# One fused VectorE instruction per score row, joint GpSimd additions and a VectorE minimum in place of TensorE mask products, in a causal attention layer

## What is computed

```python
q = (x @ Wq + bq).reshape(Bv, Tv, N_HEAD, HEAD_DIM)      # HEAD_DIM 8
k = (x @ Wk + bk).reshape(Bv, Tv, N_HEAD, LATENT)        # LATENT 64
v = (x @ Wv + bv).reshape(Bv, Tv, N_HEAD, LATENT)
qc = jnp.einsum('bthd,dl->bthl', q, Wc)
att = jnp.einsum('bthl,bshl->bhts', qc, k) * SCALE
causal = jnp.tril(jnp.ones((Tv, Tv), dtype=bool))
att = jnp.where(causal[None, None], att, -jnp.inf)
att = jax.nn.softmax(att, axis=-1)
y = jnp.einsum('bhts,bshl->bthl', att, v).reshape(Bv, Tv, N_HEAD * LATENT)
return y @ Wo + bo
```

## Time and profile before

| What | us |
|---|---|
| median of 3 runs | 3065.84 (3062.51 to 3071.13) |
| span of the profiled execution, first to last instruction | 3008.7 |
| busy in the span: PE / DVE / ACT / POOL | 2506.9 / 2417.9 / 1891.9 / 1257.2 |
| causal pairs, first to last GpSimd addition | 1344.5 to 1959.4 |
| in it, GpSimd additions (L1526) | 572.3 |
| in it, VectorE mask additions and maxima (L1775, L1777) | 150.8 and 388.0 |

### The profile page before, as it was taken

One profiled execution on the slowest core, in us unless ns is written; L12 is line 12 of the kernel. 1 busy time (PEld: TensorE's weight loads), 2 busy tenths in 40 slices (PEclk: granted clock), 3 DMA queues, 4 the chain that ended last, 5 costly groups with the idle time before them and its releaser, 6 DMA issues. The chain is left out here.

```text
span 3008.7 us, 44190 instructions
## 1 busy us (share of the span) xinstructions
PE 2506.9 (83%) x13254; PEld 1086.0 (36%) x13254; DVE 2417.9 (80%) x4200; ACT 1891.9 (63%) x3760; POOL 1257.2 (42%) x1704
## 2 busy tenths in 40 slices
PE   6897799999999899969999999996846566666666
PEld 4544122222222354424444444375821111111366
DVE  7777888888888467878888888776459999999963
ACT  2213688888888521226666666604649999999864
POOL 2015433433334101529999999911732121200036
PEclk9999899999999899979999999996979999999879
DMA  4002322222233200642222222254221111111123
GB/s 101 1 1 88 93 75 74 74 74 74 75 106 108 58 1 1 209 158 81 82 87 87 88 89 89 81 210 137 78 80 42 44 41 43 42 43 32 36 73 90
DMA packets 193930, 229.15 MB, mean 76 GB/s; under 512 B 55824, under 2 KB 122128, under 8 KB 193248
## 3 DMA queue, kind: packets, MB, share of 16 engines
q1 hardware_dynamic: 158960, 193.15, 20.0%
q0 software_dynamic: 31360, 30.05, 3.9%
q10 hardware_dynamic: 3376, 3.15, 0.4%
HBM read 139.72 MB, written 87.95 MB: 76 GB/s over the span
## 5 line engine op out<-in xcount | busy, mean ns | idle before, releaser
L1349 DVE TENSOR_REDUCE neg_max<-ps 128x1 f32<-128x1024 f32 x512 | 602.0, 1219 | 98.7 <-PE ps L1242 90.4
L1322 ACT ACTIVATE prob<-ps 128x512 f32<-128x512 f32 x1024 | 556.3, 601 | 94.3 <-PE ps L1256 85.6
L2650 DVE TENSOR_REDUCE neg_max<-ps 128x1 f32<-128x1024 f32 x512 | 581.0, 1211 | 13.8 <-PE ps L2444 13.7
L1526 POOL TENSOR_TENSOR acc<-acc,prob 128x384 f32<-128x384 f32 (+1 forms) x630 | 572.3, 952 | 34.3 <-PE ps L1620 33.2
L2520 ACT ACTIVATE ps<-ps,neg_max 128x1024 f32<-128x1024 f32 x512 | 557.4, 1091 | 23.9 <-DVE neg_max L2650 23.0
L2444 PE MATMUL ps<-k_stack,q_stack 128*128 128x512 bf16 x1024 | 332.9, 413 | 236.7 <-ACT ps L2520 216.0
L1734 ACT ACTIVATE prob<-ps 128x512 f32<-128x512 f32 (+3 forms) x640 | 270.6, 474 | 216.0 <-PE ps L1608 159.1
L1777 DVE TENSOR_REDUCE neg_max<-ps 128x1 f32<-128x512 f32 (+7 forms) x512 | 388.0, 758 | 17.5
L1256 PE MATMUL ps<-q_stack,k_stack 128*128 128x512 bf16 x1024 | 312.2, 386 | 7.1 <-DMA k_low<-k_parts 4.9
L1266 PE MATMUL ps<-prob,v 128*32 128x512 f32 x2048 | 281.3, 621 | 0.9 <-ACT prob L1322 0.7
L2444 PEld LDWEIGHTS ps<-k_stack,q_stack 128*128 128x128 bf16 x1024 | 62.6, 99 | 501.8 <-ACT ps L2520 423.2
(11 more groups left out here) (365 smaller groups left out, 3932.7 us busy)
## 6 DMA issues: line engine op xcount, KB each, us to landing
q_stack<-q_parts SPq DMA_DIRECT2D x576, 48.0 KB
k_stack<-k_parts SPq DMA_DIRECT2D x576, 48.0 KB
o_quads<-o_out SPq DMA_DIRECT2D x64, 256.0 KB
v<-v_wide SPq DMA_DIRECT2D x32, 512.0 KB
o_pairs<-o_out SPq DMA_DIRECT2D x64, 256.0 KB
num<-o_pairs SPq DMA_DIRECT2D x8, 2048.0 KB, 8.5
q_parts<-parts SPq DMA_DIRECT2D x24, 384.0 KB, 2.5
k_parts<-parts SPq DMA_DIRECT2D x24, 384.0 KB, 2.7
```

Source lines behind the costliest of these rows:

```text
L1322: nc.scalar.activation(prob[:, m % RING, :], ps[:, bank(m), :], ACT.Exp).then_inc(exped.sem, 1)
L1349: nc.vector.tensor_reduce(neg_max[:, i.slot(2), m:m + 1], ps[:, first:first + 2, :].rearrange("p b n -> p (b n)"), AX.X, ALU.max, negate=T ...
L1526: op_of.tensor_tensor(sums, sums, weights(j, u, h), ALU.add).then_inc(added_for(j, h).sem, 1)
L2650: nc.vector.tensor_reduce(neg_max[:, n % 2, qt:qt + 1], ps[:, first:first + 2, :], AX.XY, ALU.max, negate=True).then_inc(maxed.sem, 1)
```

## The change

First, a row's mask and maximum become one VectorE instruction, `tensor_tensor_reduce`: it adds a strip (`mask_strip`, 1024 columns: zeros, and the triangle in the last 128) over the row's whole width, writes the row back and puts the negated maximum out through the accumulator. Second, GpSimd adds both heads of a unit in one instruction, so 10 additions of twice the size stand where 20 stood. Third, the products with `mask_kq` are gone. The exponential of a triangle is therefore taken unmasked, and VectorE afterwards takes the minimum of it and `cap_kq` (`cap`: 0 where the key is later than the query, a huge number elsewhere), both heads at once, eight per pair. The products with the values and the additions of such a unit wait for the cap (`capped`) instead of for the exponential. For room in SBUF, `xn` of the projection now shares memory with `o_out`.

```diff
-    for m, sign in ((S.mask_qk, -1), (S.mask_kq, 1)):
-        c.run(nc.gpsimd.memset(m[:], 0.0))
-        c.run(nc.gpsimd.affine_select(out=m[:], in_=m[:], compare_op=ALU.is_ge, fill=MASKED, base=0,
+    c.run(nc.gpsimd.memset(S.mask_strip[:], 0.0))
+    c.run(nc.gpsimd.memset(S.cap_kq[:], -MASKED))
+    for m, sign, fill in ((S.mask_strip[:, SEQ - P:SEQ], -1, MASKED), (S.cap_kq[:], 1, 0.0)):
+        c.run(nc.gpsimd.affine_select(out=m, in_=m, compare_op=ALU.is_ge, fill=fill, base=0,
...
-    xn = sb("xn", [P, 2, GROUP])
+    xn = sb("xn", [P, 2, GROUP]) if xn_room is None else xn_room
...
+    BOTH = slice(0, 2)
+    diagonals = [u for u, (kt, c) in enumerate(units) if kt * P >= c * GROUP]
+    CAPS = len(diagonals)
+    caps_after = {1: (0,), 4: (2,), 6: (4,), 9: (6,), 12: (8, 9), 15: (10,)}
+    adds_after = {6: (2, 4), 9: (4, 6), 12: (6, 8), 15: (8, 10)}
+
+    def wait_for_weights(eng, j, u, h):
+
+        if u in diagonals:
+            capped.wait(eng, j.times(CAPS, diagonals.index(u)))
+        else:
+            exped.wait(eng, j.times(2 * NU, 2 * u + h))
...
-    def add(eng, op_of, j, u, h):
+    def add(eng, op_of, j, u, heads):
         kt, c = units[u]
-        exped.wait(eng, j.times(2 * NU, 2 * u + h))
+        last = 1 if heads == BOTH else heads
+        wait_for_weights(eng, j, u, last)
...
-                op = nc.tensor.matmul(ps[:, bank(t, j.c), o:GROUP], ks[j.slot(4)][:, h, kt * P:(kt + 1) * P],
-                                      qs[j.slot(4)][:, h, c * GROUP + o:(c + 1) * GROUP], start=True,
-                                      stop=not diagonal)
-                if diagonal:
-                    op = nc.tensor.matmul(ps[:, bank(t, j.c), o:o + P], S.ident_b[:], S.mask_kq[:],
-                                          start=False, stop=True)
-                op.then_inc(s2_mm.sem, 1)
+                nc.tensor.matmul(ps[:, bank(t, j.c), o:GROUP], ks[j.slot(4)][:, h, kt * P:(kt + 1) * P],
+                                 qs[j.slot(4)][:, h, c * GROUP + o:(c + 1) * GROUP], start=True,
+                                 stop=True).then_inc(s2_mm.sem, 1)
...
-                exped.wait(pe, j.times(2 * NU, 4 * couple + 3))
                 for u in (2 * couple, 2 * couple + 1):
+                    wait_for_weights(pe, j, u, 1)
...
+            def cap(j, u):
+                exped.wait(dve, j.times(2 * NU, 2 * u + 1))
+                triangles = weights(j, u, BOTH)[:, :, 0:P]
+                nc.vector.tensor_tensor(triangles, triangles, bcast_heads(S.cap_kq[:]), ALU.min
+                                        ).then_inc(capped.sem, 1)
+
             def step(i, n):
                 for m in range(NQ):
+                    if m == 1 and there(n, 3):
+                        cap(i - 3, NU - 1)
                     if there(n, 0):
...
-                        nc.vector.tensor_tensor(own, own, S.mask_qk[:], ALU.add).then_inc(qk_masked, 1)
-                        dve.wait_ge(qk_masked, i.times(NQ, m + 1))
-                        nc.vector.tensor_reduce(neg_max[:, i.slot(2), m // KTS, qt:qt + 1],
-                                                ps[:, bank:bank + c + 1, :].rearrange("p b n -> p (b n)")
-                                                [:, 0:(qt + 1) * P],
-                                                AX.X, ALU.max, negate=True).then_inc(maxed.sem, 1)
+                        width = (qt + 1) * P
+                        row = ps[:, bank:bank + (width - 1) // GROUP + 1, :].rearrange("p b n -> p (b n)")[:, 0:width]
+                        nc.vector.tensor_tensor_reduce(row, row, S.mask_strip[:, SEQ - width:SEQ], scale=-1.0,
+                                                       scalar=-MASKED, op0=ALU.add, op1=ALU.min,
+                                                       accum_out=neg_max[:, i.slot(2), m // KTS, qt:qt + 1]
+                                                       ).then_inc(maxed.sem, 1)
+                    if m in caps_after and there(n, 2):
+                        for u in caps_after[m]:
+                            cap(i - 2, u)
+                        if n - 2 == NP - 1 and m >= 6:
+                            for u in range(*adds_after[m]):
+                                add(dve, nc.vector, i - 2, u, 1)
...
                     for u in range(FIRST, NU):
-                        for h in (0, 1):
-                            if h == 0 or n - 2 < NP - 1:
-                                add(pool, nc.gpsimd, i - 2, u, h)
+                        add(pool, nc.gpsimd, i - 2, u, BOTH if n - 2 < NP - 1 else 0)
```

More of the change, by code:

```diff
@@ L1482, in attend_pairs @@
     sums_out = sb("sums_out", [P, GROUP])
[L1483 to L1484 removed]
+    (s1_mm, maxed, split, m_mm, m_read, s2_mm, exped, capped, pv_mm, added, last_added, also_added, sum_mm, sum_read, o_read0, o_read1) = [
+        steps(n) for n in ("s1_mm maxed split m_mm m_read s2_mm exped capped pv_mm added last_added also_added sum_mm sum_read o_read0 "
                            "o_read1").split()]
@@ L1513, in wait_for_added @@
         if j.c < NP - 1:
-            added.wait(eng, j.times(ADDS, 2 * n + h))
+            added.wait(eng, j.times(ADDS, n))
         else:
             added_for(j, h).wait(eng, n)
-    def add(eng, op_of, j, u, h):
+    def add(eng, op_of, j, u, heads):
         kt, c = units[u]
-        exped.wait(eng, j.times(2 * NU, 2 * u + h))
+        last = 1 if heads == BOTH else heads
+        wait_for_weights(eng, j, u, last)
         if kt == 1:
-            pv_mm.wait(eng, j.times(2 * NU, 2 * c + h))
+            pv_mm.wait(eng, j.times(2 * NU, 2 * c + last))
         else:
-            wait_for_added(eng, j, units.index((kt - 1, c)) - FIRST, h)
-        sums = acc[:, j.slot(2), h, c, offset(u):GROUP]
-        op_of.tensor_tensor(sums, sums, weights(j, u, h), ALU.add).then_inc(added_for(j, h).sem, 1)
+            wait_for_added(eng, j, units.index((kt - 1, c)) - FIRST, last)
+        sums = acc[:, j.slot(2), heads, c, offset(u):GROUP]
+        op_of.tensor_tensor(sums, sums, weights(j, u, heads), ALU.add).then_inc(added_for(j, last).sem, 1)
     def wait_for_bank(pe, what, c):
@@ L1772, in step @@
                         s1_mm.wait(dve, i.times(NQ, m))
-                        c, at = divmod(qt * P, GROUP)
-                        own = ps[:, bank + c, at:at + P]
-                        nc.vector.tensor_tensor(own, own, S.mask_qk[:], ALU.add).then_inc(qk_masked, 1)
-                        dve.wait_ge(qk_masked, i.times(NQ, m + 1))
-                        nc.vector.tensor_reduce(neg_max[:, i.slot(2), m // KTS, qt:qt + 1],
-                                                ps[:, bank:bank + c + 1, :].rearrange("p b n -> p (b n)")
-                                                [:, 0:(qt + 1) * P],
-                                                AX.X, ALU.max, negate=True).then_inc(maxed.sem, 1)
+                        width = (qt + 1) * P
[10 more added lines that the diff above has]
+                                add(dve, nc.vector, i - 2, u, 1)
+                    if m == 10 and n == NP:
+                        early.invert(dve)
+                if n - 3 == NP - 1:
+                    add(dve, nc.vector, i - 3, NU - 2, 1)
+                    add(dve, nc.vector, i - 3, NU - 1, 1)
             run(dve, step)
-            early.invert(dve)
-            for u in range(FIRST, NU):
-                add(dve, nc.vector, Head(0, NP - 1), u, 1)
         def gpsimd(pool):
@@ L1869, in attend_pairs @@
     ahead = Shared()
-    return attach, ahead, v_room
+    return attach, ahead, v_room, o_out
 def quads_of(S):
```

16 lines of the change are left out of this document (9 added, 7 removed).

## The result

The changed kernel takes 3171.52 us (median of 4 runs, 3169.12 to 3177.46) where the kernel before, timed on the same chip, takes 3064.42: a ratio of 1.0347, 95% interval 1.0331 to 1.0364. It is 107 us slower.

The account below looks back on a forecast made before the run. It took a ring of in-order queues as the bound, GpSimd nearest to full. A pair grows 2.8 us, 19.50 to 22.3; 31 pairs add 87 us, the last pair 2: 3065.8 becomes 3155, range 3036 to 3223.

Parts of the forecast that it names:

- the chain of a pair: Additions and caps in turn between GpSimd and VectorE, summed over one pair: 23.0 us, or 21.6, against 19.50.
- the rule by which a cap gets its turn: VectorE's cap beside GpSimd's additions: waits until GpSimd has nothing ready, then ends some 0.29 us later.
- The rival of free caps: Caps run unhindered and TensorE's saved 0.96 us decides: a pair of 18.54 us, 3036 us in all; chance 0.18.
- The likeliest case: The sum for one pair with held caps: 22.3 us, 2.8 above 19.50, 3155 us in all; chance 0.50.
- accumulator read: Second VectorE instruction after each fused mask and maximum: 0.1 us taken, 1.6 us a pair (0 to 3.1).
- get in between additions 8 and 9: The cap of unit 10 might run before GpSimd's addition 9, making the pair 21.6 instead of 23.0 us.
- the 6.96 us row: VectorE's first addition in the last pair, 384 columns, beside eight unbroken GpSimd additions; undisturbed it would take 0.55 us.
- one addition only: A cap waits for one GpSimd addition and precedes the next: a pair of 20.2 us, 3089 us; chance 0.18.
- Joint additions: GpSimd adds both heads at once: 16.7 us a pair with overlap, a gain of 1.4 us there.
- The mask products: Sixteen 128-column products a pair on TensorE at 0.06 us each: 0.96 us, inside the sum and returning as waiting.
- the ring: In-order engine queues waiting on one another; no engine alone the bound of a 19.50 us pair, GpSimd nearest to full.
- 57 us lie outside: The gap between the profiled 3008.7 us and the median 3065.8, assumed to stay the same around the changed kernel.

Follow-up runs that it names:

- five ready: Kernel before with joint additions; in the last pair GpSimd starts once five additions are ready, VectorE its own after GpSimd's first: 3068.57 us.
- the filled spells: Changed kernel with eight TensorE products of zeros a pair, placed where TensorE stood idle before the value products of units 10 and 11: 3149.33 us, ratio 1.0264.
- the kernel with the masks back: Changed kernel with TensorE's mask products put back and the caps taken out, fused rows and joint additions kept: 3055.65 us, ratio 0.9954.
- masks in PSUM: Changed kernel without caps or mask products; VectorE adds the mask to 16 score triangles a pair in PSUM before the exponential: 3132.94 us, ratio 1.0219.

## Why the prediction was right, and where not

**The direction, the cause and the chain of a pair hold; the rule by which a cap gets its turn does not, and the halved clock was missing.** By parts, in us a pair, each from two kernels that differ in it:

```
kernel before                                    19.50
joint additions alone (-> 19.49)                 -0.01
fused rows (19.49 -> 19.33)                      -0.16
mask products away (19.33 -> 18.57)              -0.76
caps with one SBUF input (18.57 -> 18.70)        +0.13
their second SBUF input, full clock (-> 22.05)   +3.35
halved clock (-> 23.07)                          +1.02
```

The caps' second SBUF input costs 3.35 us, and 4.37 with the halved clock that comes with it, where the gains of the change are 0.93. With additions of one head the pair is 21.11, so some 2.41 of the 3.35 would be there without joint additions, and 0.94 is theirs. The rival of free caps priced the other side rightly: a pair of 18.54, measured 18.70 and 18.57. The likeliest case had 22.3 and is 22.05 where the clock is full.

**The sum, item by item,** from the end of one cap to the end of the next, in the pair of 22.05 us shown above:

```
                              predicted  measured
to the cap of unit 4            4.52      4.50
to the cap of unit 6            3.98      3.93
to the caps of units 8 and 9    3.85      3.73
to the cap of unit 10           4.64      4.45
to the cap of unit 11           1.65      1.62
to the next cap of unit 2       4.40      3.82
                               23.04     22.05
```

The items behind GpSimd hold to 0.2 us. The last one, VectorE's own, is 0.58 too long, 0.4 of it by the **accumulator read**, the term that was mis-sized: it takes 138 ns, near the 0.1 taken, but the next instruction mostly starts at the same time as the read (1639.25 and 1639.25), so sixteen of them cost next to nothing and not 1.6 us a pair. The rest is that an instruction of VectorE starts some 0.08 us before the one ahead ends (1639.25 for the row behind the one that ends at 1639.33). The cap of unit 10 did not get in between additions 8 and 9; I had halved between 23.0 and 21.6, so that 22.3 came nearer to 22.05 than the reasoning deserved: that was luck.

**The rule for a cap was wrong.** "It waits until GpSimd has nothing ready" rested on the 6.96 us row. A cap waits for the one addition that runs: 1.50 us at most beside additions of one head that follow without a break, 1.55 us with five ready. In the changed kernel the two rules give the same: a cap frees two additions, VectorE comes to the next cap during the second, and then the second is also the last. That the two rules agree here was luck too. The cap of unit 4 shows how little decides: VectorE came to it at 1639.50, and the second addition had begun at 1639.44. It came late because the row ahead of it waited 0.65 us for TensorE's scores, at 1638.23. By how much an earlier arrival would shorten the pair wasn't tried.

**The rival "one addition only" had the right rule and a wrong price.** It let both engines share the time without loss, 20.2 us. They don't: while a cap waits, VectorE's rows wait behind it, and when GpSimd is through, it waits for the cap (64.7 us of 500). The same rule gives 21.11 us with additions of one head and 22.05 with joint ones. The page "SBUF — State Buffer" of the Trainium skill, section "Who interferes with whom", lets the engine that comes second wait for one whole instruction; every cap in these traces agrees. All 158 caps of the changed kernel that were held, and all 214 with additions of one head, end 0.28 to 0.29 us behind the end of the addition that ran when VectorE came to them; the one shown at 1639.50, of 2.58 us, had 2.30 left of a joint addition. The same section says that a VectorE reduction never contends on this chip; 224 of at most 0.421 us agree. The rows of 6.96 and 7.41 us, which are no caps, do not agree and stay unexplained; the error was to make a rule for caps of them.

**Joint additions** were to gain 1.4 us a pair on GpSimd, 1.2 by the busy times of the kernel with them alone, and I called this gain hidden in the chain. Beside caps it is worse, by the 0.94 us above. At the full clock (the filled spells) the eight caps of a pair take 9.9 us, five of them held, and GpSimd waits 4.4 us a pair for caps; with additions of one head they take 8.5 us, seven of them held, and GpSimd waits 1.3.

**The mask products** cost 0.048 us each and not 0.06, the time from start to start that I had taken; and the chain hides 0.66 of the 0.76, as the prediction said. Taking them out of the kernel with the masks back brought 0.76 us a pair, where over 3 us less on VectorE and 1.2 less on GpSimd had brought 0.17: TensorE bounded the pair, and not the ring or GpSimd, "the nearest to full".

**What was missing is TensorE's clock.** Nothing before showed anything but 1.00 there, and the prediction didn't ask what TensorE's waits would do to it. It makes 1.02 us a pair, about 31 us, which is more than the 16.5 by which 3155 fell short of 3171.5: 22.3 taken for 22.05 gave 8 us of it back, and most of the rest lies in the first two pairs, which were counted at 2.8 us each and hardly grew.

**The base** was the median, so the shorter execution shown before did no harm; that "57 us lie outside", in the prediction's sum and in the section on the profile before, was wrong: it is 2.

## What to carry to other kernels

Before an operation moves to VectorE, look where its inputs lie and what GpSimd does at that time: with two inputs in SBUF beside GpSimd's additions its price here was its own time and up to one whole addition, and longer additions raised that limit (1.50 us with 512 columns, 2.58 with 1024); an instruction of the same width with one SBUF input cost its own time, 0.42 us. A gain on an engine is worth what the bound engine leaves of it: 1.2 us a pair on GpSimd and over 3 on VectorE brought 0.01 and 0.16 us here, since TensorE was full. And where a change makes TensorE wait in spells of about a microsecond, read the granted clock of the stretch before anything else.

## What the hardware showed that I had not expected

- In the changed kernel TensorE's granted clock goes to half, the 1.2 GHz level, behind two idle spells of 0.98 and 0.97 us with 0.65 us of products between them, in about half of the pairs, and comes back after some 7 us; products 512 wide then take 0.63 instead of 0.38 us. With masks in PSUM, TensorE had idle spells of 0.94 and 0.43 us in every pair, and the granted clock stayed at 1.00, the 2.4 GHz level. Why only some pairs with the two long spells lose it, these runs don't show.
- The fused mask and maximum runs at the maximum's rate, 1.239 us for 1024 columns, and its accumulator read (0.138 us) lies beside the next instruction.
- An addition of VectorE took 7.41 and 6.96 us beside eight or more of GpSimd's in two executions of the kernel before. With five ready additions it took 1.55. The cause is open.
